# One mask product a head, float32r experts in the first feed-forward stage, and a rebuilt step order in the fourth attention

## The chip, the cores and the metric

The kernel runs on one core of one Trainium2 chip. The metric is the device time of one launch in microseconds (us). One core has five engines that work side by side and meet at semaphores: TensorE (PE in the rows), VectorE (DVE), ScalarE (ACT), GpSimd (POOL) and SyncE (SP, which issues DMAs).

## The reference, cut to what matters

Four transformer layers run one behind the other on x of shape (8, 256, 256): attention, normalisation, feed-forward, normalisation. The change touches three of the attentions and the first feed-forward stage.

```python
def _L0_ffn_ref(...):                       # 32 experts, 8 taken per token
    scores = jax.nn.sigmoid(logits)         # top 2 of 4 groups, then top 8 experts
    ...
    x_lat = x @ fc1_w.T
    h = relu2(jnp.einsum('tl,eil->eti', x_lat, w1))
    h = h * cw.T[:, :, None]
    y_lat = jnp.einsum('eti,eli->tl', h, w2)
    routed = y_lat @ fc2_w.T
    shared = relu2(x @ shared_up_w.T) @ shared_down_w.T
    return (shared + routed).reshape(orig_shape)

def _L1_attn_ref(...):                      # 16 heads of 128, causal
    scores = jnp.einsum('bhqd,bhkd->bhqk', q, k) * scale
    scores = jnp.where(mask[None, None], -jnp.inf, scores)
    attn = jax.nn.softmax(scores, axis=-1)
    ...

def _L3_attn_ref(...):                      # 16 heads, two score maps each, causal
    energy = jnp.einsum('bqhad,bkhad->bahqk', qd, kd)
    energy = jnp.where(causal, NEG, energy)
    scores = jax.nn.softmax(energy / np.sqrt(D), axis=-1)
    diff = scores[:, 0] - lam * scores[:, 1]
    diff = jnp.where(causal, NEG, diff)
    diff = jax.nn.softmax(diff, axis=-1)    # a second softmax
    att = jnp.einsum('bhqv,bvhd->bqhd', diff, v)
    att = att * jax.lax.rsqrt(jnp.mean(att * att, axis=-1, keepdims=True) + EPS) * rms_w
    return (att * (1.0 - LAM_INIT)).reshape(b, s, E) @ Wo
```

## The kernel before, in words

There are eight stages, named l0a, l0f, l1a, l1f, l2a, l2f, l3a and l3f (layer, then attention or feed-forward). x stays in SBUF as `x_sb`; between two stages a boundary normalises it and transposes it into `xT`. In each stage every engine has a program of its own, written by hand, and the order of the work is the order in which these programs are written, with semaphore waits between them.

**The masks.** A score tile of a head holds 128 query rows of the first half of the sequence against 128 keys, and 128 rows of the second half against 256 keys. The causal mask is added inside PSUM by a bf16 matrix product of the identity with a 128x128 mask tile: two products a head, of 128 columns each (L290 in l0a, L950 in l1a, L1836 in l3a). In l1a they stand between the score products (L948) of a group of two heads; there are 64 groups.

**l0f.** The 2048 tokens go in four chunks of 512, and each chunk runs over the 32 experts. For expert e, PE makes `hidden` = w1[e] times the latent tokens (L645, float32, which the trace records as two passes), and a product that spreads the expert's token weights over all partitions (L648, bf16). ScalarE takes relu (L687) and square (L689), VectorE multiplies by the weights (L757), and PE adds w2[e] times the result to the chunk's sum (`latent`, L652, float32), two experts behind. Before this loop stand the token routing (a long chain on VectorE) and the shared expert.

**l3a.** A batch of 256 tokens is handled in 8 steps, i=0 to i=7. A step makes one score map of 8 of the 32 (L1832), its maxima (VectorE L2090), its exponentials (ScalarE L1984, in two pairs of heads), and works on earlier maps: the ratio of the two softmaxes (L2097 to L2099), scaling, difference and mask (GpSimd L1947, L1950, L1937), the second maxima (L2106, L2108), the second exponentials (`second`, L2004), the transposes (`turn`, L1847) with their copies out of PSUM (L1995, L2116), the products with the values (L1857, L1860), the turning back (L1867) and the copy of the result (`take_output`, L2127). In between stand "pieces" for the next batch: projections (L1767, L1774, L1782) with their rotations on VectorE (L2055, L2058). Once a batch, the result of the batch before is squared (GpSimd L1954), normalised by three Newton steps on 128x32 tiles (L81 to L88) and a product (L2140), transposed (L1874), copied (L2010), projected (L1882), added to x (L108) and measured for the normalisation that follows (L115 to L121). Each engine's `sequence` function sets the order of a step; `live` says which parts exist while the pipeline fills and drains. `b` is the batch of the score maps, `piece_out` counts the pieces that VectorE has rotated, `on_raw` the results that it has taken.

## Time and profile before

| | |
|---|---|
| median of 3 runs | 3006.09 us (3003.32 to 3007.58) |
| the profiled execution | 2994.62 us, span 2992.8 us |
| PE busy | 2497.6 us (83%), mean granted clock 0.934 of full speed |
| VectorE busy | 1854.3 us (62%) |
| ScalarE busy | 1356.1 us (45%) |
| GpSimd busy | 461.8 us (15%) |
| l0f's expert loop | about 345 to 610 us of the span |
| l1a | about 660 to 1400 us |
| l3a | about 1957 to 2487 us |

Times in the rows are microseconds from the start of the span. The clock column of a stretch is TensorE's granted clock as a share of full speed. Busy shares are means over stages with different limits, so each stage has to be read by itself.

### The profile page before, as it was taken

The numbers are of one execution on the slowest core, as the hardware profiler recorded it, in microseconds if no ns is written. First come the engines' busy times: TensorE is split into PE (matmuls) and PEld (weight loads), VectorE is DVE, ScalarE is ACT, GpSimd is POOL, SyncE is SP. The second block draws the span as 40 slices with busy tenths as digits, with TensorE's granted clock in tenths as the row PEclk, the third lists the DMA queues.
The fourth block names the chain that finished last, engine by engine and source line by source line (L and its number), as shares of the span: only waits on it lengthen the run. The fifth ranks groups of instructions, "written<-read, shape, count | busy, mean of one in ns | idle before, by whom it ended". The sixth has DMA issues, their size and how long they took to land. (4 is left out here: it accounts for less than half of the span.)

```text
span 2992.8 us, 43034 instructions
## 1 busy us (share of the span) xinstructions
PE 2497.6 (83%) x14256; PEld 1870.0 (62%) x14256; DVE 1854.3 (62%) x4212; ACT 1356.1 (45%) x3688; POOL 461.8 (15%) x398
## 2 busy tenths in 40 slices
PE   7998999979999999995998786766666655999997
PEld 5665544457777777775676565654444434877876
DVE  3665333355675566756445757567777775777777
ACT  4664455554454444543222222267776762322332
POOL 2441000010000000000121000046565550000000
PEclk9998999989999999998999888889898866999999
DMA  4002000001110011102000000100000003000000
GB/s 154 7 11 85 1 0 0 0 4 32 32 32 17 14 32 32 32 21 105 1 0 0 0 0 0 35 17 4 7 4 4 4 1 138 1 0 0 0 0 28
DMA packets 28080, 63.74 MB, mean 21 GB/s; under 512 B 4208, under 2 KB 16496, under 8 KB 26480
## 3 DMA queue, kind: packets, MB, share of 16 engines
q1 hardware_dynamic: 28016, 62.93, 6.0%
q8 instruction: 35, 0.57, 0.1%
q14 instruction: 29, 0.24, 0.0%
HBM read 54.27 MB, written 2.10 MB: 19 GB/s over the span
## 5 line engine op out<-in xcount | busy, mean ns | idle before, releaser
L1984 ACT ACTIVATE l3a_pr<-psum,l3a_nm 128x128 f32<-128x128 f32 (+1 forms) x512 | 206.1, 420 | 90.5 <-DVE l3a_nm L2090 90.5
L757 DVE TENSOR_TENSOR l0f_hg<-l0f_sq,psum 128x512 f32<-128x512 f32 x128 | 87.7, 687 | 151.1 <-ACT l0f_sq L689 148.4
L108 DVE TENSOR_TENSOR x_sb<-psum,x_sb 128x512 f32 (+2 forms) x48 | 41.7, 868 | 219.7 <-PE psum L984 104.9
L2344 ACT ACTIVATE l3f_sg<-psum 128x512 f32<-128x512 f32 x96 | 57.3, 597 | 240.3 <-PE psum L2300 240.3
L1045 ACT ACTIVATE l1a_pr<-psum,l1a_nb,l1a_rq 128x128 f32<-128x128 f32 (+1 forms) x256 | 127.3, 510 | 85.2 <-DVE l1a_nb L1131 81.1
L2297 PE MATMUL psum<-l3f_x_hi,l3f_w_hi 128*128 x384 | 154.5, 402 | 8.6 <-DVE l3f_w_lo L2380 8.6
L2298 PE MATMUL psum<-xT,l3f_w_hi 128*128 x384 | 152.8, 398 | 0.0
L2299 PE MATMUL psum<-l3f_x_hi,l3f_w_lo 128*128 x384 | 152.1, 396 | 0.0
L2004 ACT ACTIVATE l3a_pr<-l3a_pr,l3a_nb,l3a_rec 128x128 f32<-128x128 f32 (+1 forms) x256 | 119.4, 542 | 68.5 <-DVE l3a_nb L2108 68.5
L1847 PE MATMUL psum<-cf_sb,l3a_pr 128*128 128x128 f32 x384 | 73.6, 312 | 82.3 <-ACT l3a_pr L2004 82.3
L2090 DVE TENSOR_REDUCE l3a_nm<-psum 128x2 f32<-128x256 f32 (+1 forms) x256 | 124.6, 548 | 24.5 <-PE psum L1836 21.8
L1305 POOL TENSOR_TENSOR l1f_acc<-l1f_t 128x512 f32<-128x512 f32 x4 | 6.3, 1573 | 855.7 <-DVE l1f_t L1368 855.7
L948 PE MATMUL psum<-l1a_kT,l1a_qT 128*128 128x128 f32 (+1 forms) x512 | 118.6, 355 | 21.0 <-ACT l1a_pr L1045 14.0
L2311 PE MATMUL psum<-l3f_w_hi,l3f_h_hi 128*128 128x256 f32 x384 | 126.5, 329 | 7.9 <-DVE l3f_h_lo L2398 7.9
L1947 POOL TENSOR_TENSOR l3a_pr<-l3a_pr,l3a_ratio 128x256 f32<-128x256 f32 (+1 forms) x128 | 103.2, 828 | 193.0 <-DVE l3a_ratio L2099 193.0
L1937 POOL TENSOR_TENSOR l3a_pr<-l3a_pr,w_l3a_mask 128x1024 f32<-128x1024 f32 x32 | 75.7, 2365 | 368.9 <-ACT l3a_pr L1984 368.9
L652 PE MATMUL psum<-l0f_hg,w_l0f_w 128*128 128x512 f32 x256 | 130.5, 593 | 0.8 <-DVE l0f_hg L757 0.8
L645 PE MATMUL psum<-l0f_xl,w_l0f_w 128*128 x256 | 130.6, 592 | 0.0
L687 ACT ACTIVATE l0f_relu<-psum 128x512 f32<-128x512 f32 x128 | 76.3, 596 | 108.7 <-PE psum L645 104.3
L374 POOL TENSOR_TENSOR l0a_pr<-l0a_pr,l0a_rec 128x256 f32<-128x256 f32 (+1 forms) x128 | 101.9, 828 | 144.2 <-DVE l0a_rec L464 144.2
L2391 DVE TENSOR_TENSOR l3f_gu<-l3f_sg,psum 128x512 f32<-128x512 f32 x96 | 66.0, 688 | 89.5 <-ACT l3f_sg L2344 89.5
L2328 ACT ACTIVATE l3f_w_hi<-w_l3f_all 128x768 fp32r<-128x768 f32 x97 | 82.2, 848 | 80.5 <-PE psum L2313 78.8
(445 smaller groups left out, 7198.9 us busy)
## 6 DMA issues: line engine op xcount, KB each, us to landing
l1a_kT<-l1a_o_dram SPq DMA_DIRECT2D x64, 256.0 KB, 2.7
w_l3f_all<-l3f_all_dram SPq DMA_DIRECT2D x1, 9216.0 KB, 25.7
w_l0f_w<-l0f_w_dram SPq DMA_DIRECT2D x2, 2048.0 KB, 10.1
w_l1f_all<-l1f_all_dram SPq DMA_DIRECT2D x1, 2560.0 KB, 9.5
cf_sb<-xT SPq DMA_DIRECT2D x9, 256.0 KB, 2.5
x_sb<-x_dram SPq DMA_DIRECT2D x1, 2048.0 KB, 8.6
l0a_xc<-xT SPq DMA_DIRECT2D x8, 256.0 KB, 2.5
w_l1a_q<-l1a_q_dram SPq DMA_DIRECT2D x1, 2048.0 KB, 8.1
```

The costliest lines, as they stand in the source:

```text
L645: mm(HB[e % 3], w["w1"][:, e, :], xl[:, chunk], start=True, stop=True).then_inc(h_ps, 1)
L652: mm(YL, w["w2"][:, e, :], hg[:, e % 2, :], start=(e == 0), stop=(e == E - 1)).then_inc(used, 1)
L948: mm(S[n % 2][:, i, t * P:t * P + (t + 1) * P], qT[:, h, t * P:(t + 1) * P], kT[:, h, 0:(t + 1) * P], start=True, stop=False)
L1045: last = nc.scalar.activation(pr[:, n % 2, i, s], S[n % 2][:, i, s], ACT.Exp, bias=nb[:, n % 2, t, i:i + 1], scale=rq[:, t, 2 * n + i:2 * ...
L1947: last = nc.gpsimd.tensor_tensor(pr[:, r, 1, heads, k], pr[:, r, 1, heads, k], bc(ratio[:, r, heads, t], 2, (t + 1) * P), ALU.mult)
L1984: last = nc.scalar.activation(pr[:, r, a, g, k], S[:, g, k], ACT.Exp, bias=nm[:, i % 2, g, t:t + 1], accum_out=sums[:, r, a, g, t:t + 1])
L2004: last = nc.scalar.activation(pr[:, r, 1, g, k], pr[:, r, 0, g, k], ACT.Exp, bias=nb2[:, r, g, t:t + 1], scale=rec[:, r, 0, g, t:t + 1])
L2090: last = nc.vector.tensor_reduce(nm[:, i % 2, 2 * pair:2 * pair + 2, t], S[:, 2 * pair:2 * pair + 2, t * P:t * P + (t + 1) * P], AX.X, ALU ...
L2297: mm(bk[e % 2], hi, x_hi[:, k, chunk], start=(k == 0), stop=False)
L2298: mm(bk[e % 2], hi, x_lo[:, k, chunk], start=False, stop=False)
L2299: mm(bk[e % 2], lo, x_hi[:, k, chunk], start=False, stop=(k == KD - 1))
L2311: mm(Y[:, t, :], h_hi[:, e % 2, tokens], hi, start=False, stop=False)
```

## The change

Six things are done together.

1. Each head's two mask products become one of 256 columns: its output is a view of the bank, `diagonals(bank)`, that holds both diagonal blocks. In l1a the four score products of a group now come first and its two mask products last.
2. In l0f, w1 and w2, the latent tokens and the gated hidden values are split into a float32r part (`_hi`) and its remainder (`_lo`), and each float32 product becomes three float32r products: hi·hi, hi·lo and lo·hi. w's hi parts are made by ScalarE between the steps of the shared expert (8 pieces of 128x1024), the lo parts by GpSimd (8 pieces), xl_hi by ScalarE, xl_lo by VectorE (4 products ahead of the top-k chain). In the loop relu, square and the multiplication work in place in four buffers `act_h`; h_hi of even experts is copied by ScalarE, that of odd ones by VectorE; h_lo is a VectorE subtraction. `latent` runs three experts behind instead of two.
3. To make room, l1a's v weights (2 MB) are loaded in the boundary ahead of l1a instead of one boundary earlier, third in the queue behind q and k.
4. In l3a VectorE makes the second maxima right behind the maxima. The sums of the norm stand at i=5, the Newton steps and the product in i=6 ahead of its copy out of PSUM, and their `rs` lies in PSUM, so that each Newton operation reads at most one operand from SBUF. Squares move from i=3 to i=2.
5. In l3a the output projection of a batch, its addition to x and its measure move from i=7 of the next batch to i=0 and i=1 of the batch after that. ScalarE's copy `output` comes behind both pairs of exponentials instead of between them.
6. In l3a the pieces move: queries 3 from i=0 to i=3, values from i=4 to i=5, queries 2 from i=6 to i=7; the piece stands ahead of both transposes instead of between them, and at i=4 the turning back stands between the two transposes, with its result taken at the end of the same step.

```diff
-                        for t in range(TT):
-                            last = mm(S[:, g, 2 * t * P:(2 * t + 1) * P], c["idb"], c["maskb"], start=False, stop=(t == TT - 1))
+                        last = mm(diagonals(S[:, g, :]), c["idb"], bc(c["maskb"], 1, TT), start=False, stop=True)
...
                     def hidden(e):
                         if e >= 3:
-                            pe.wait_ge(sq_ready, b * E + e - 2)
-                        mm(HB[e % 3], w["w1"][:, e, :], xl[:, chunk], start=True, stop=True).then_inc(h_ps, 1)
+                            pe.wait_ge(relu_ready, b * E + e - 2)
+                        mm(HB[e % 3], w_hi["w1"][:, e, :], xl_hi[:, chunk], start=True, stop=False)
+                        mm(HB[e % 3], w_hi["w1"][:, e, :], xl_lo[:, chunk], start=False, stop=False)
+                        mm(HB[e % 3], w_lo["w1"][:, e, :], xl_hi[:, chunk], start=False, stop=True).then_inc(h_ps, 1)
...
+                        nc.scalar.activation(act_h[:, e % 4, :], act_h[:, e % 4, :], ACT.Square).then_inc(sq_ready, 1)
+                        if e % 2 == 1:
+                            act.wait_ge(hg_ready, b * E + e)
+                            if e >= 4:
+                                act.wait_ge(used, b * E + e - 3)
+                            nc.scalar.activation(h_hi[:, (e - 1) % 3, :], act_h[:, (e - 1) % 4, :], ACT.Copy).then_inc(hhi_even, 1)
...
+                        nc.vector.tensor_tensor(act_h[:, e % 4, :], act_h[:, e % 4, :], GB[e % 2], ALU.mult).then_inc(hg_ready, 1)
+                        if e >= 1:
+                            low(e - 1)
+                        if e % 2 == 1:
+                            dve.wait_ge(hg_ready, b * E + e + 1)
+                            if e >= 3:
+                                dve.wait_ge(used, b * E + e - 2)
+                            nc.vector.tensor_copy(h_hi[:, e % 3, :], act_h[:, e % 4, :]).then_inc(hhi_odd, 1)
...
-        rs = sb("rs", [P, TT * H])
+        rs = PT[1][:, 3 * P:3 * P + TT * H]
...
                 def sequence(b, opening=False, second_pass=False, closing=False, more=True):   # VectorE
+                    behind = not (opening or second_pass)
                     for i in range(NU):
                         if not closing:
                             maxima(b, i)
                             if i == 7 and more:
-                                add_keys(b * NQ + 8)
+                                add_keys(b * NQ + 7)
+                        if live(i, 3, opening, closing):
+                            second_maxima(b, i)
                         if i % 2 == 0 and live(i, 1, opening, closing):
                             ratios(b, i)
                         if i % 2 == 0 and live(i, 6, opening, closing):
                             values_out(b, i)
-                        if i % 2 == 1 and live(i, 7, opening, closing):
+                        if i == 0 and behind:
+                            output(b - 2)
+                        if i in (1, 3, 7) and live(i, 7, opening, closing):
                             if i == 7 and not opening:
                                 dve.wait_ge(on_ready, b)
                             take_output(b, i)
-                        if not closing and i < 7:
+                        if not closing:
                             piece_in(b, i, more)
+                        if i == 5 and not opening:
+                            norm_1(b - 1)
                         if live(i, 4, opening, closing):
                             out_of_psum(b, i, opening)
-                        if live(i, 3, opening, closing):
-                            second_maxima(b, i)
-                        if not opening:
-                            if i == 6:
-                                norm_1(b - 1)
-                                norm_2(b - 1)
-                            if i == 7:
-                                output(b - 1)
-                                dve.wait_ge(z_ready, b + 1)
-                                measure(nc, st, x_sb, mv, b * TT - TT, TT, lw)
+                        elif i == 6 and closing:
+                            norm_2(b - 1)
+                        if i == 4 and not opening:
+                            take_output(b, i)
+                        if i == 1 and behind:
+                            dve.wait_ge(z_ready, b - 1)
+                            measure(nc, st, x_sb, mv, b * TT - 2 * TT, TT, lw)
```

How the change moves instructions is shown at three places. First PE in l0f's expert loop, from one expert's weight product to the next; `w_l0f_w` and `l0f_w_hi`, `l0f_w_lo` are the weights, `l0f_c3T` the token weights. Before:

```order
L648 MATMUL psum<-l0f_c3T,w_l0f_sel 128x512
L652 MATMUL psum<-l0f_hg,w_l0f_w 128x512
L645 MATMUL psum<-l0f_xl,w_l0f_w 128x512
L647 REGISTER_ALU
L648 MATMUL psum<-l0f_c3T,w_l0f_sel 128x512
```

Now:

```order
L666 MATMUL psum<-l0f_c3T,w_l0f_sel 128x512
L670 MATMUL psum<-l0f_h_hi,l0f_w_hi 128x512
L671 MATMUL psum<-l0f_h_hi,l0f_w_lo 128x512
L672 MATMUL psum<-l0f_h_lo,l0f_w_hi 128x512
L661 MATMUL psum<-l0f_xl_hi,l0f_w_hi 128x512
L662 MATMUL psum<-l0f_xl_lo,l0f_w_hi 128x512
L663 MATMUL psum<-l0f_xl_hi,l0f_w_lo 128x512
...
L666 MATMUL psum<-l0f_c3T,w_l0f_sel 128x512
```

One float32 product of 512 columns has become three float32r products, twice for each expert.

Second, VectorE in l3a's looped pass, at the end of step i=6 and in i=7. Before:

```order
L2106 TENSOR_REDUCE l3a_nm<-l3a_pr 128x2 x2
...
L2108 TENSOR_TENSOR l3a_nb<-l3a_nm,l3a_rec 128x4
L2134 TENSOR_REDUCE l3a_vv<-l3a_osq 128x32
...
L81 TENSOR_SCALAR l3a_rs<-l3a_vv 128x32
...
L84 TENSOR_TENSOR l3a_tmp<-l3a_rs 128x32
...
L2140 TENSOR_TENSOR l3a_on<-l3a_raw,l3a_rs 128x512
...
L2090 TENSOR_REDUCE l3a_nm<-psum 128x2 x2
...
L2065 TENSOR_TENSOR l3a_kr<-l3a_k 128x512
L2127 COPY l3a_raw<-psum 128x8x17
L2116 COPY l3a_pt<-psum 128x384
L2106 TENSOR_REDUCE l3a_nm<-l3a_pr 128x2 x2
...
L108 TENSOR_TENSOR x_sb<-psum,x_sb 128x512
```

Now (L2167 are the maxima, L2183 and L2185 the second ones, L2217 to L2222 the norm):

```order
L2167 TENSOR_REDUCE l3a_nm<-psum 128x2 x2
...
L2183 TENSOR_REDUCE l3a_nm<-l3a_pr 128x2 x2
...
L2185 TENSOR_TENSOR l3a_nb<-l3a_nm,l3a_rec 128x4
...
L2200 COPY l3a_ots<-psum 128x256
L2217 TENSOR_SCALAR psum<-l3a_vv 128x32
...
L2219 SCALAR_TENSOR_TENSOR l3a_tmp<-psum,l3a_vv 128x32
...
L2222 TENSOR_TENSOR l3a_on<-l3a_raw,psum 128x512
L2195 COPY l3a_pt<-psum 128x384
...
L2167 TENSOR_REDUCE l3a_nm<-psum 128x2 x2
...
L2183 TENSOR_REDUCE l3a_nm<-l3a_pr 128x2 x2
...
L2185 TENSOR_TENSOR l3a_nb<-l3a_nm,l3a_rec 128x4
L2206 COPY l3a_raw<-psum 128x8x17
```

The norm's operations have moved ahead of the copy L2195, the second maxima stand right behind the maxima, and the addition to x (L108) is gone from i=7.

Third, PE in the same pass, in i=7 and at the start of the next batch. Before:

```order
L1832 MATMUL psum<-l3a_kr,l3a_qr 128x128 x4
L1832 MATMUL psum<-l3a_kr,l3a_qr 128x256 x4
L1836 MATMUL psum<-cb_sb 128x128 x8
L1847 MATMUL psum<-cf_sb,l3a_pr 128x128 x3
L1874 MATMUL psum<-cf_sb,l3a_on 128x128 x4
L1847 MATMUL psum<-cf_sb,l3a_pr 128x128 x3
L1882 MATMUL psum<-l3a_wo,l3a_oT 128x256 x4
```

Now:

```order
L1888 MATMUL psum<-l3a_kr,l3a_qr 128x128 x4
L1888 MATMUL psum<-l3a_kr,l3a_qr 128x256 x4
L1891 MATMUL psum<-cb_sb 128x2x128 x4
L1902 MATMUL psum<-cf_sb,l3a_pr 128x128 x6
L1929 MATMUL psum<-cf_sb,l3a_on 128x128 x4
L1834 MATMUL psum<-xT,w_l3a_q 128x256 x4
...
L1888 MATMUL psum<-l3a_kr,l3a_qr 128x128 x4
```

The output projection (L1882) has left i=7, and a projection of queries (L1834) has come there, behind the transposes and ahead of the next batch's scores.

## Rows read from the trace of the kernel before

**Rows 1.** Busy time by stretch: span, PE, weight loads, VectorE, ScalarE, GpSimd, clock, DMA.

```profile
345.00:610.00 265.00, 255.60 (x666) 113.03 (x665) 101.03 (x169) 156.47 (x256) 0.00 (x0) 1.00 0.00 0
```

**Rows 2.** The same view for one batch of l3a and its closing pass.

```profile
2065.90:2129.00 63.10, 40.28 (x384) 29.14 (x383) 48.73 (x115) 44.85 (x172) 37.56 (x29) 0.91 0.01 4
...
2445.30:2487.00 41.70, 21.10 (x102) 13.49 (x101) 17.62 (x58) 14.07 (x39) 7.91 (x7) 0.57 0.00 0
```

**Rows 3.** Waits in l3a, 2012.9 to 2445.3: total us, times, longest.

```profile
ACT l3a_pr L1984 <- DVE l3a_nm L2090: 65.5, 15, 6.8
ACT l3a_pr L2004 <- DVE l3a_nb L2108: 57.2, 49, 2.2
```

**Rows 4.** Timeline of one plain step of l3a: start, us, [idle before <-releaser].

```profile
2159.40 0.35 ACT L1984 ACTIVATE l3a_pr<-psum,l3a_nm 128x128 f32<-128x128 f32 x1
...
2161.86 0.69 DVE L2058 TENSOR_TENSOR l3a_qr<-psum,w_l3a_rope_q 128x512 f32<-128x512 f32 x1 [1.99 <-PE psum L1774]
...
2162.74 0.94 PE L1832 MATMUL psum<-l3a_kr,l3a_qr 32*128 32x128 f32 x16 [0.60 <-ACT l3a_pr L1984]
...
2163.97 0.16 DVE L2108 TENSOR_TENSOR l3a_nb<-l3a_nm,l3a_rec 128x4 f32<-128x4 f32 x1
2164.08 1.95 DVE L2090 TENSOR_REDUCE l3a_nm<-psum 128x2 f32<-128x256 f32 x4
...
2164.16 1.86 ACT L2004 ACTIVATE l3a_pr<-l3a_pr,l3a_nb,l3a_rec 128x128 f32<-128x128 f32 x4 [1.09 <-DVE l3a_nb L2108]
...
2165.93 0.35 ACT L1984 ACTIVATE l3a_pr<-psum,l3a_nm 128x128 f32<-128x128 f32 x1
```

**Rows 5.** Timeline around the norm of one batch, VectorE, GpSimd and PE apart.

```profile
2184.89 1.68 DVE L84 TENSOR_TENSOR l3a_tmp<-l3a_rs 128x32 f32<-128x32 f32 x1
2186.61 2.26 DVE L86 SCALAR_TENSOR_TENSOR l3a_tmp<-l3a_vv,l3a_tmp 128x32 f32<-128x32 f32 x1
...
2189.13 0.19 DVE L84 TENSOR_TENSOR l3a_tmp<-l3a_rs 128x32 f32<-128x32 f32 x1
...
2198.11 0.69 DVE L108 TENSOR_TENSOR x_sb<-psum,x_sb 128x512 f32 x1 [2.68 <-PE psum L1882]
...
2186.49 2.33 POOL L1937 TENSOR_TENSOR l3a_pr<-l3a_pr,w_l3a_mask 128x1024 f32<-128x1024 f32 x1
...
2191.23 1.12 PE L1874 MATMUL psum<-cf_sb,l3a_on 128*128 128x128 f32 x4 [5.12 <-DVE l3a_on L2140]
...
2194.49 3.46 PE L1882 MATMUL psum<-l3a_wo,l3a_oT 128*128 128x256 f32 x8 [1.50 <-ACT l3a_oT L2010]
```

**Rows 6.** Timeline of l0f's expert loop.

```profile
599.78 0.60 ACT L687 ACTIVATE l0f_relu<-psum 128x512 f32<-128x512 f32 x1 [0.68 <-PE psum L645]
...
600.66 1.02 PE L645 MATMUL psum<-l0f_xl,w_l0f_w 128*128 x2
...
601.13 0.69 DVE L757 TENSOR_TENSOR l0f_hg<-l0f_sq,psum 128x512 f32<-128x512 f32 x1 [1.25 <-ACT l0f_sq L689]
...
602.60 1.02 PE L645 MATMUL psum<-l0f_xl,w_l0f_w 128*128 x2
```

**Rows 7.** Timeline of l3f, which already has float32r products and roundings.

```profile
2704.69 0.40 PE L2297 MATMUL psum<-l3f_x_hi,l3f_w_hi 128*128 x1
...
2704.92 0.43 DVE L2396 CAST l3f_h_hi<-l3f_hw 128x512 fp32r<-128x512 f32 x1
...
2705.38 0.69 DVE L2398 TENSOR_TENSOR l3f_h_lo<-l3f_hw,l3f_h_hi 128x512 fp32r<-128x512 f32 x1
2705.39 0.40 PE L2297 MATMUL psum<-l3f_x_hi,l3f_w_hi 128*128 x1
...
2705.99 0.95 DVE L2380 TENSOR_TENSOR l3f_w_lo<-w_l3f_all,l3f_w_hi 128x768 fp32r<-128x768 f32 x1
```

**Rows 8.** Timeline of PE in one group of l1a: its first score product, and what follows.

```profile
705.17 0.39 PE L948 MATMUL psum<-l1a_kT,l1a_qT 128*128 128x128 f32 x2
...
706.87 0.82 PE L959 MATMUL psum<-cf_sb,l1a_pr 128*128 128x128 f32 x6
```

More of the change, by code:

```diff
@@ L1822, in scores @@
+                def scores(b, i, opening, more):
                     r, a = i // A, i % A
@@ new lines, in sequence @@
+                            if i in (2, 4) and more and not closing:
+                                pe.wait_ge(piece_out, b * NQ + (6 if i == 2 else 8))
+                            if i == 6:
+                                pe.wait_ge(piece_out, b * NQ + (11 if more else 7))
+                            values(b, i)
+                        if i == 0 and behind:
+                            if closing:
+                                pe.wait_ge(on_raw, b * R - 3)
+                            else:
+                                pe.wait_ge(piece_out, b * NQ + 5)
+                            project_output(b - 2)
@@ L1896, in sequence @@
+                        if not closing and i < 7:
+                            piece(b, i, opening, more)
                         if turning:
                             turn(b, i, 0)
[L1898 to L1911 removed]
@@ L2145, in output, with sequence @@
                     add_output(nc, x_sb, b * TT, TT, OB.rearrange("p (t n) -> p t n", t=TT), z_ready)
-                def sequence(b, opening=False, closing=False, more=True):
+                def sequence(b, opening=False, second_pass=False, closing=False, more=True):
+                    behind = not (opening or second_pass)
                     for i in range(NU):
```

299 lines of the change are left out of this document (183 added, 116 removed).

## Prediction

> **What bounds the kernel now.** I read the busy times by stretch first, since the three parts of the change lie in stages with different limits. In l0f's expert loop [rows 1] PE is busy for 255.6 of 265 us at the full clock while ScalarE has 156.5 and VectorE 101.0: PE is the bound. The timeline says how: one expert's first product starts at 600.66 and the next one's at 602.60, so an expert takes 1.94 us [rows 6], and both other engines wait in it for PE or for each other.
>
> In l3a nobody is full. One batch takes 63.1 us, with VectorE busy for 48.7, ScalarE 44.9, PE 40.3 and GpSimd 37.6 [rows 2]. So I looked at the waits: from 2012.9 to 2445.3, ScalarE waits 65.5 us for the first maxima in 15 waits of up to 6.8, and 57.2 us for the second maxima (L2108) in 49 short ones [rows 3]. These are two different faults.
>
> The short one stands in a plain step, which lasts 6.53 (from 2159.40 to 2165.93) [rows 4]. VectorE has the next score maxima only after second maxima that stand behind a rotation, which waited 1.99 for PE's projection; ScalarE then idles 1.09 before its second exponentials, which end just when the next step begins.
>
> The long ones come once a batch, at the norm [rows 5]. The Newton steps stand ahead of the maxima of i=7. Two 128x32 operations take 1.68 and 2.26 beside GpSimd work (L1937 runs from 2186.49 for 2.33), and the same operation takes 0.19 at 2189.13, once GpSimd is done. PE has by then stood still for 5.12. After that the output projection takes 3.46 for 8 products, VectorE waits 2.68 for it in L108, and the score products of the next batch stand behind it. This is the second of the waits of several us.
>
> **l0f, part by part.** An expert had two float32 products and a bf16 one, and gets six float32r products and the bf16 one. In l3f three float32r products of 512 columns take 0.70 (from 2704.69 to 2705.39), 0.233 each [rows 7]. Seven make 1.63 against 1.94: 0.31 less, times 128 experts 39.7.
>
> Do the others keep up? VectorE gets, for two experts, two multiplications, two subtractions and a cast. A subtraction lasts 0.69 in its record, but the next instruction starts 0.61 behind it (2705.38 to 2705.99), and the cast lasts 0.43 [rows 7]. By starts it is 4 x 0.61 + 0.46 = 2.90, by whole records 4 x 0.69 + 0.43 = 3.19, that is 1.45 or 1.60 an expert. ScalarE's 256 instructions were busy for 156.5 [rows 1], 0.61 each; five for two experts are 1.53 an expert. Both are under 1.63, so PE stays the bound, but barely: all three are within 12%. I take 1.63, with 1.70 as the worse end (a wait of 0.14 in each pair), which costs 9 us.
>
> At a chunk's end the last expert's chain is laid bare. It gains a cast (0.46), its own subtraction (0.61) and the subtraction of the expert before it that stands ahead (0.61), and gets back 0.3 on shorter products: about +1.3, four times, 5.2. Ahead of the loop ScalarE rounds the weights in 8 pieces of 1024 columns between the steps of the shared expert. At 0.61 for 512 columns they are 9 us of work; PE has three banks ahead of ScalarE there, so I take +1 of it as shown, between 0 and 9. And VectorE's four subtractions go ahead of a routing chain. GpSimd's 8 pieces of the weights run beside that chain; it is the one place where the change puts GpSimd work beside VectorE work that had none. If that chain grew by up to 5 us, it would still end ahead of the shared expert, which PE finishes; if that cover were gone, 5 us would show. Sum for l0f: -39.7 + 5.2 + 1 = -33.5, between -17 (the worse end of each) and -40.
>
> **l3a, the plain steps.** With second maxima right behind the maxima, ScalarE's work for its second exponentials is ready while it makes the first ones. What is left of a step is a loop over ScalarE, PE and VectorE: exponentials and the way to PE 3.34 (2159.40 to 2162.74), score products 0.87, half the mask products 0.16, half of the maxima 0.93 to 1.0 and the way to ScalarE, together 2.3 [rows 4]. That is 5.65 for a step, 45.2 for a batch: the floor. ScalarE itself needs 44.9/8 = 5.6, VectorE 48.7/8 = 6.1 less the stalls in its own records (3.6 a batch), so 5.65 too [rows 2, 5]. Three engines are then at one level, and any wait in order shows.
>
> I went through the new order step by step and put each step at the floor or at what comes late. At i=0 the turning back waits for the addition to x, which waits for the projection (+0.6). At i=1 VectorE also measures (+0.4). At i=2 the turning back waits for a rotation of keys (+0.6). At i=3 PE has two projections, and the second waits for a result taken in the same step by VectorE: the next scores come late (+1.5). i=4 is +0.3, i=5 with the norm's sums and two pieces +1.1. At i=6 VectorE has Newton's ten operations (about 2.2 at the 0.19 of [rows 5] with the gaps between them) and the product: +1.9. At i=7 the projection of queries 2 waits for a result that VectorE takes behind the sum of the keys, and stands ahead of the next batch's scores: +2.4. The sum is 45.2 + 8.8 = 54.0, against 63.1: -9.1, for seven batches -64. Where the additions are all half as large, a batch is 49.6; where the waits at i=3, i=7 and i=0 are twice as large, 58.5. The first batch has no norm and gains only from the plain order, about -3. In the closing pass, 41.7 us at a mean clock of 0.57 [rows 2], the last ratio no longer stands behind the addition to x and its 2.68 of waiting [rows 5]; but the moved projections must still be made. I take -7, between 0 and -10. Sum for l3a: -74, between -40 and -105.
>
> **The norm and GpSimd, weighed.** The rows show a factor of 9 to 12 between the same operation beside GpSimd work and without it [rows 5]. They do not show whether operands in PSUM help. With `rs` in PSUM I cost the Newton steps at the free price; if they don't help, they cost 3.6 more in each of seven batches, +25. The Trainium skill, "SBUF — State Buffer", section "Who interferes with whom", says that a VectorE instruction with two SBUF inputs contends with a GpSimd instruction that reads SBUF, and that with at most one it does not; the trace agrees for the two inputs (1.68 and 2.26 against 0.19), and for the single input no row here shows it. The same rule speaks against the change where two SBUF inputs stay: the sum of the keys, the second operation of the norm's sums, L2185, and the routing of l0f beside the new GpSimd work. By it the Newton steps are free and these may each cost up to one GpSimd instruction.
>
> **The masks and the rest.** A group's four score and four mask products take 1.70 (705.17 to 706.87) [rows 8]. Their columns alone need 1.28 (768 float32 columns, at 0.85 for 512: half of the 1.94 that is left without the bf16 product) and 0.23 for 512 bf16 ones, so 0.19 is lost between eight products. The edit saves at most that in a group, at least nothing; I take 0.09 for 64 groups: -5.5, between 0 and -12. In l0a the same edit stands off the limiting chain: -0.3. The later load of v is third in its queue, and ScalarE and PE are still on q and k when it lands; I take 0, and 8 us if it isn't hidden.
>
> **Sum.** -33.5 - 74 - 5.5 - 0.3 = -113. From the profiled execution's 2994.6 that gives 2881. The median of the runs shown is 11.5 higher; scaled to it, 2893.
>
> **The rivals.**
> - The new waits of PE in l3a (i=3, i=7, i=0) are as large as the old ones, and a batch takes 58 to 61. For it: PE waits for VectorE in the same step three times, where it waited once. Against it: the 5.12 and 3.46 are gone from the path. At 59.5 l3a gives -36, all -75: about 2931, or 2917 at 57.5. Chance 0.25.
> - The steps reach nearly the floor, 49 to 50.5: l3a -105, all -144: 2862. Chance 0.15.
> - The stall stays although `rs` lies in PSUM: +25, 2918. Chance 0.04.
> - l0f becomes bound by VectorE and ScalarE at 1.70 or more: 2902 to 2906. It is within my own range. Chance 0.08.
> - Slower or no change: TensorE gets its lower level, half the clock, in l0f's loop. A product then costs 0.47, an expert 3.3. At that price the gain of 113 is gone once about 0.53 of the 128 experts run so (113/(128 x 1.66)). In its favour, the float32r products last barely longer than the others need; against it, PE had 1.00 there and stays busy [rows 1]. Chance 0.03.
> - My forecast, a batch of 52 to 57 and an expert at 1.61 to 1.66: 2872 to 2912. Chance 0.45.
>
> **The numbers.** 2893 is the likeliest. The two ends come from the first two rivals: 2855 and 2935 leave out about 0.15. A median can be told from no change at about 0.2%, 6 us here. Faster 0.97, within it 0.01, slower 0.02.
>
> **What would show it.** In the profile after: an expert's first products 1.63 apart with PE over 95% busy, or 1.70 with gaps; l3a's batches from i=7 to i=7 at 54 with ScalarE's waits for first maxima spread over i=3, i=6 and i=7, none above 3; its waits for L2185 near zero; Newton operations at 0.2 beside running GpSimd work; an output projection at i=0 that no engine waits for by more than 1. The prediction is wrong if batches stay above 58, if the second maxima now wait for GpSimd's difference, or if l0f's experts are over 1.75.

## The result: 0.978 of the time before, half to six tenths of the gain that was forecast

The changed kernel takes 2937.5 us in the median of 4 runs (2936.46 to 2944.65), and the kernel before 3004.7 in the median of the runs beside it: a ratio of 0.9777 with a 95% interval of 0.9759 to 0.9794. It is faster, by 67 us. The forecast was 2893, in a range of 2855 to 2935, so the measured time lies just outside. By the medians that is six tenths of the 113 that were forecast. The profiled executions are 2994.62 and 2937.16 us, 57.5 apart, which is half of it; the one of before is 11.5 under its median.

Where the 57.5 came from can be read from the first and last starts of the same products in both traces. l1a's first score product starts at 654.9 instead of 681.7: l0f gave 26.8 (forecast 33.5). From l1a's first to its last score product it is 666.1 instead of 671.8: 5.7 (forecast 5.5). From l3a's first score product to l3f's first expert product it is 547.8 instead of 570.1: 22.3, where 74 were forecast. The stages between and behind have the rest, under 3. The miss is in l3a. Inside these 22.3, by the starts of the first exponentials, the first batch gave 0.9, the six batches behind it 8.4 together, the last one, up to its i=7, 6.6, and what follows up to l3f 6.3. So seven batches gave 15 us where 64 were forecast.

The stretches of the profile after, one chunk of l0f's loop, the start of the next, and one batch of l3a; the columns are those of [rows 1]:

```profile
345.40:403.20 57.80, 55.43 (x233) 38.07 (x232) 48.51 (x82) 45.80 (x80) 0.00 (x0) 1.00 0.00 1
403.20:408.30 5.10, 2.98 (x13) 1.75 (x11) 3.88 (x14) 2.35 (x4) 0.00 (x0) 1.00 0.00 0
408.30:414.00 5.70, 5.66 (x18) 3.79 (x18) 4.44 (x8) 4.61 (x8) 0.00 (x0) 0.70 0.00 0
...
2162.20:2223.60 61.40, 43.90 (x349) 31.14 (x349) 48.84 (x114) 44.20 (x169) 37.93 (x29) 0.83 0.01 4
```

A batch of l3a takes 61.4 us instead of 63.1 [rows 2], with the same work on VectorE and ScalarE and TensorE's mean granted clock at 0.83 instead of 0.91. The waits from 1978 to 2400, nearly seven batches, in the columns of [rows 3]:

```profile
ACT l3a_pr L2059 <- DVE l3a_nm L2167: 86.0, 55, 4.7
PE psum L1834 <- DVE l3a_raw L2206: 45.6, 13, 5.2
...
PE psum L1922 <- DVE l3a_ots L2200: 30.9, 16, 2.7
...
ACT l3a_pr L2079 <- DVE l3a_nb L2185: 5.8, 6, 1.0
```

The waits for the second maxima are gone (5.8 instead of 57.2), as the change meant them to be. But ScalarE waits for its first maxima by 86.0 instead of 65.5, now in 55 waits instead of 15. And there is a new row: PE waits 45.6 for the copy L2206 ahead of the projection of queries L1834, once at i=7 and once at i=3 of nearly every batch. The worst place is i=7, in time order:

```profile
2211.00 1.94 DVE L2167 TENSOR_REDUCE l3a_nm<-psum 128x2 f32<-128x256 f32 x4
2211.67 0.60 PE L1929 MATMUL psum<-cf_sb,l3a_on 128*128 128x128 f32 x4
...
2212.86 2.12 DVE L2138 TENSOR_TENSOR l3a_kr<-l3a_k 128x512 f32<-128x512 f32 x1
2214.38 2.79 POOL L2012 TENSOR_TENSOR l3a_pr<-l3a_pr,w_l3a_mask 128x1024 f32<-128x1024 f32 x1
2214.90 1.00 DVE L2183 TENSOR_REDUCE l3a_nm<-l3a_pr 128x2 f32<-128x256 f32 x2
...
2215.93 1.27 DVE L2185 TENSOR_TENSOR l3a_nb<-l3a_nm,l3a_rec 128x4 f32<-128x4 f32 x1
2217.12 0.29 DVE L2206 COPY l3a_raw<-psum 128x136 f32<-128x136 f32 x1
...
2217.46 3.78 PE L1834 MATMUL psum<-xT,w_l3a_q 128*128 x8 [5.20 <-DVE l3a_raw L2206]
2221.18 1.03 PE L1888 MATMUL psum<-l3a_kr,l3a_qr 32*128 32x128 f32 x16
```

VectorE has the maxima at 2212.9, then makes the sum of the keys in 2.12 us, the second maxima, L2185 in 1.27, and only then the copy of 0.29 for which PE waits. PE stands still for 5.20, and its projection then takes 3.78 for 8 products. The scores of the next batch come behind it, at 2221.18. From the first exponentials of i=7 to those of i=0 it is 11.57 us (2212.05 to 2223.62).

### The profile page after: what moved, and what is told of

Read it like the earlier page. It is cut to its first block and busy times, and to the rows that moved or that the text cites. A ratio compares the mean times of both kernels' runs of the same rounds, so it can differ in the third digit from the quotient of the medians.

```text
span 2935.4 us, 42983 instructions
## 1 busy us (share of the span) xinstructions
PE 2473.6 (84%) x14000; PEld 1912.8 (65%) x14000; DVE 1958.4 (67%) x4408; ACT 1389.4 (47%) x3760; POOL 483.6 (16%) x406
## 5 line engine op out<-in xcount | busy, mean ns | idle before, releaser
L2167 DVE TENSOR_REDUCE l3a_nm<-psum 128x2 f32<-128x256 f32 (+1 forms) x256 | 124.7, 550 | 50.5 <-PE psum L1891 50.1
L1834 PE MATMUL psum<-xT,w_l3a_q 128*128 (+1 forms) x256 | 84.2, 488 | 48.8 <-DVE l3a_raw L2206 47.9
L1007 PE MATMUL psum<-l1a_kT,l1a_qT 128*128 128x128 f32 (+1 forms) x512 | 100.6, 342 | 22.7 <-ACT l1a_pr L1105 15.7
L1044 PE MATMUL psum<-l1a_kT,l1a_ko 128*128 128x256 f32 x512 | 112.6, 381 | 6.1 <-ACT l1a_ko L1094 6.1
L2025 POOL TENSOR_TENSOR l3a_pr<-l3a_pr 128x768 f32<-128x768 f32 x64 | 115.7, 1808 | 5.0
L1635 PE MATMUL psum<-w_l2f_down,l2f_hh 128*128 128x256 f32 x256 | 73.5, 457 | 47.9 <-DVE l2f_hh L1703 47.9
L2059 ACT ACTIVATION_READ_ACCUMULATOR l3a_pr<-psum,l3a_nm 128x1 f32 x512 | 110.6, 216 | 0.0
```

The lines of the kernel that those rows point to most:

```text
L1044: last = mm(PT[0][:, t * D:(t + 1) * D], oT[:, h, t * P:(t + 1) * P], wo[:, h, :], start=(h == 0), stop=(h == H - 1))
L2025: nc.gpsimd.tensor_tensor(pr[:, r, 0, heads, :], pr[:, r, 0, heads, :], pr[:, r, 1, heads, :], ALU.add).then_inc(dif_ready, 1)
L2059: last = nc.scalar.activation(pr[:, r, a, g, k], S[:, g, k], ACT.Exp, bias=nm[:, i % 2, g, t:t + 1], accum_out=sums[:, r, a, g, t:t + 1])
L2167: last = nc.vector.tensor_reduce(nm[:, i % 2, 2 * pair:2 * pair + 2, t], S[:, 2 * pair:2 * pair + 2, t * P:t * P + (t + 1) * P], AX.X, ALU ...
```

## The experiments

The times of before beside the experiments were 3003.6 to 3006.0 in the median. Ratios are those to before of the same chip. Twelve kernels ran.

**1. The parts apart.** The changed kernel with the fourth attention's old order, so with l0f and the masks alone. The edit exchanges the whole function `l3_attention` for that of the kernel before, with one mask product a head.

> The changed kernel with the fourth attention's old order (its mask products stay merged). It leaves the gains of l0f and of the masks. The trace of the changed kernel has l1a's first score product 26.8 us earlier and l1a itself 5.7 us shorter. If the parts are additive: 3004.7 - 26.8 - 5.7 - 2 = about 2970, and the step order of l3a is worth about 32 us less than nothing else: 2937 - 2970 = -33. If l3a's rebuilt order is worth only what lies between its first score product and l3f (22 us), this kernel takes 2960.

Measured: 2972.4 us (2965.4 to 2974.2), ratio 0.9894 (0.9877 to 0.9910). The forecast of 2970 holds. l0f and the masks are worth 32 us, and the rebuilt order of l3a the other 35. The 22 us that the two profiled executions gave for l3a are no contradiction: from l3a's first score product to l3f's first expert product the old order takes 570.1 in the trace of before and 576.9 in the trace of this kernel, so single executions of the same order differ by 7 us.

**2. The masks alone,** on the kernel before; the cut shows l0a and l3a, and in l1a the two mask products of a group also move behind its four score products:

```diff
-                        for t in range(TT):
-                            last = mm(S[:, g, 2 * t * P:(2 * t + 1) * P], c["idb"], c["maskb"], start=False, stop=(t == TT - 1))
+                        last = mm(diagonals(S[:, g, :]), c["idb"], bc(c["maskb"], 1, TT), start=False, stop=True)
```

> The kernel before with only the merged mask products in l0a, l1a and l3a. Theory: 5.7 us in l1a, nothing in l0a, and in l3a little, since ScalarE and VectorE set its step: 2998, a gain of 5 to 9. Rival: in l3a the scores reach VectorE 0.2 us earlier in each of 64 steps, another 13: 2986.

Measured: 2994.5 us (2984.0 to 3002.6), ratio 0.9965 (0.9945 to 0.9985): 4 to 17 us. The forecast 2998 lies in it, the rival's 2986 just outside. It is faster. In its trace l1a, from its first to its last score product, is 6.6 us shorter than before, while l3a is 10.7 longer up to l3f's first expert product, so nothing here shows that l3a gained.

**3. The copy first.** The changed kernel, with VectorE's copy right behind the maxima at i=3 and i=7, nothing else moved (the second hunk takes it out of its old place):

```diff
                         if not closing:
                             maxima(b, i)
-                            if i == 7 and more:
-                                add_keys(b * NQ + 7)
+                        if i in (3, 7) and live(i, 7, opening, closing):
+                            if i == 7 and not opening:
+                                dve.wait_ge(on_ready, b)
+                            take_output(b, i)
+                        if i == 7 and more and not closing:
+                            add_keys(b * NQ + 7)
                         if live(i, 3, opening, closing):
                             second_maxima(b, i)
...
-                        if i in (1, 3, 7) and live(i, 7, opening, closing):
-                            if i == 7 and not opening:
-                                dve.wait_ge(on_ready, b)
+                        if i == 1 and live(i, 7, opening, closing):
                             take_output(b, i)
```

> The changed kernel, but at i=3 and i=7 of l3a VectorE takes the turned-back result right behind the maxima, ahead of the sum of the keys and the second maxima. Theory 'order': the batch of 61.45 us is long because PE's projection at i=7 waits 5.2 us (and at i=3 1.1 us) for that copy, then runs at the lower clock (3.78 instead of 1.99) ahead of the next scores. The copy comes about 4.3 and 2.3 us earlier, so a batch loses 5 to 6.5: 2892 to 2902. Theory 'ports': the sum of the keys (2.12 us) and L2185 (1.27) stay as long beside GpSimd work and hold the next maxima instead: at most 1.5 a batch, 2927 or more.

Measured: 2888.6 us (2885.0 to 2892.5), ratio 0.9611 (0.9593 to 0.9630). That is 49 us less than the changed kernel, from the place of one instruction of 0.29 us in two of eight steps. A batch is down from 61.4 to 54.75: i=7 is 4.4 shorter, i=3 2.3, and the other steps are as they were within 0.2. The place at i=7 now reads:

```profile
2131.14 1.94 DVE L2167 TENSOR_REDUCE l3a_nm<-psum 128x2 f32<-128x256 f32 x4
2132.18 0.37 ACT L2059 ACTIVATE l3a_pr<-psum,l3a_nm 128x128 f32<-128x128 f32 x1 [1.78 <-DVE l3a_nm L2167]
2132.99 0.29 DVE L2206 COPY l3a_raw<-psum 128x136 f32<-128x136 f32 x1
2133.20 1.92 DVE L2138 TENSOR_TENSOR l3a_kr<-l3a_k 128x512 f32<-128x512 f32 x1
...
2133.34 1.99 PE L1834 MATMUL psum<-xT,w_l3a_q 128*128 x8 [1.08 <-DVE l3a_raw L2206]
...
2135.56 0.94 PE L1888 MATMUL psum<-l3a_kr,l3a_qr 32*128 32x128 f32 x16 [0.23 <-ACT l3a_pr L2059]
```

The sum of the keys is nearly as slow as it was (1.92 instead of 2.12), yet PE no longer waits for it. PE waits 1.08 instead of 5.20, its projection takes 1.99 instead of 3.78, and the scores wait for ScalarE's exponentials by 0.23, as they should. The mean clock of a batch is 0.94. Theory "order" holds, and theory "ports" falls: with the stalls still there the batch lost 6.7, not 1.5. That the stalls cost nothing at all doesn't follow: i=7 still takes 7.2, and the maxima of the next step start at 2138.34, behind these operations, while PE's mask products ended at 2137.04.

**4. Two of the three stalls beside GpSimd taken away instead,** on the changed kernel. L2185 becomes four operations with one SBUF input and a scalar each, and the norm's second operation reads one input from PSUM. For this the norm's sums also move behind the wait for the transpose. The third stall, that of the sum of the keys, stays:

```diff
-                    nc.vector.tensor_tensor(nb2[:, r, heads, :], nm2[:, r, heads, :], rec[:, r, 0, heads, :], ALU.mult).then_inc(nb_ready, 1)
+                    for g in range(heads.start, heads.stop):
+                        for t in range(TT):
+                            last = nc.vector.tensor_scalar(nb2[:, r, g, t:t + 1], nm2[:, r, g, t:t + 1], rec[:, r, 0, g, t:t + 1], None, ALU.mult)
+                    last.then_inc(nb_ready, 1)
...
-                    st.do(nc.vector.tensor_reduce(by_head(vv[:, :]), osq[:, :, :, 0:HD], AX.X, ALU.add))
+                    st.do(nc.vector.tensor_reduce(by_head(tv), osq[:, :, :, 0:HD], AX.X, ALU.add))    # tv in PSUM, vv in SBUF
```

> The changed kernel, but L2185 (two SBUF inputs, 1.27 to 1.35 us beside GpSimd work, 0.16 alone) is made of four operations with one SBUF input and a scalar each, and the norm's second operation (2.24 us at i=5, 0.21 alone) reads one input from PSUM. Theory 'ports': the waits of 1.1 at i=7, 1.2 at i=3 and 2.0 at i=5 go, 4 us a batch, 2908 to 2915. Theory 'order': only what brings the copies at i=3 and i=7 forward counts, 2.3 less 0.3 for three more operations, 2921 to 2926. Should the operations with one input be stalled too, no change.

Measured: 2939.7 us (2938.3 to 2940.4), ratio 0.9782 (0.9765 to 0.9798): no gain. The two stalls themselves did go. The four operations and the norm's second one over the whole run:

```profile
L2188 DVE TENSOR_SCALAR l3a_nb<-l3a_nm,l3a_rec x256: 202/204/216, 1947.3 to 2413.6; 128x1 f32<-128x1 f32 x128
...
L2220 DVE SCALAR_TENSOR_TENSOR l3a_vv<-l3a_osq,psum x8: 204/208/210, 2018.7 to 2422.5; 128x32 f32<-128x32 f32 x8
```

The longest of 256 is 216 ns, and the norm's operation has 208 ns in the median, where the changed kernel has 2233. But four operations last 0.58 together where the one lasted 0.16 unless it was stalled, in every one of 64 steps, and PE still waits 4.46 for the copy at i=7, behind the sum of the keys at 2.12. So the equal time is a sum of gains and prices, and not a proof that the stalls were free. In most batches of the trace i=3 takes 7.7 instead of 8.5 and i=1 is 0.3 shorter, while i=0, i=2 and i=6, where L2185 had taken its 0.16, are 0.4 longer each; the mean batch is 61.5 in both kernels. What the stall of the sum of the keys costs in this order was not measured by itself.

**5. Both edits together:**

> Both edits of the two runs before: copies first at i=3 and i=7, and L2185 and the norm's second operation with one SBUF input. With the long wait gone, the batch is 54.75 us and VectorE stands on more of its steps, so a stall of VectorE should now show. Theory 'ports show once the order is mended': the 2.24 at i=5 becomes 0.2 and L2185's stalls go: 2 to 3 us a batch, 2868 to 2875. Rival: as in the changed kernel, where the same edit gave nothing, the time is in PE's waits: 2885 to 2892.

Measured: 2895.7 us (2895.4 to 2896.1), ratio 0.9642 (0.9612 to 0.9672). By the medians that is 7 us more than experiment 3, against my expectation, but the two ran on different chips and the intervals of their ratios overlap, so a loss isn't shown. In the trace the steady batches are in fact shorter: the third to the seventh take 54.0, 55.2, 53.6, 52.6 and 53.9 us, where experiment 3 has 54.7 each time. i=0, i=2 and i=6 are 0.4 longer, which is the price of the four operations, but i=7 is 0.7 shorter and i=5 takes 5.7 in four of the five, where experiment 3 has 7.1 to 7.6. So by the trace the stalls do cost something once the order is mended: 0.9 a batch beyond the price of the four operations.

What is longer is the second batch (55.5 instead of 53.2) and the last (50.4 instead of 45.4). At i=3 of the last one PE waits for its copy about as long in both kernels, but the projection behind the wait takes 3.78 here:

```profile
2324.86 3.78 PE L1835 MATMUL psum<-xT,w_l3a_q 128*128 128x256 f32 x8 [1.82 <-DVE l3a_raw L2212]
```

and 1.99 in experiment 3:

```profile
2323.56 1.99 PE L1834 MATMUL psum<-xT,w_l3a_q 128*128 128x256 f32 x8 [2.03 <-DVE l3a_raw L2206]
```

The granted clock behind the wait is 0.50 here and 1.00 there. Why it differs isn't shown.

**6. Keep PE busy through the wait.** The changed kernel with unread products ahead of the wait at i=7:

```diff
                     if i == 7 and more:
+                        for _ in range(40):
+                            mm(PT[1][:, 4 * P - 64:4 * P], c["idb"], c["maskb"][:, 0:64], start=True, stop=True)
                         pe.wait_ge(on_raw, b * R + 1)
```

> The changed kernel with 40 small bf16 products that nobody reads, put by PE at i=7 of l3a ahead of its wait for the copy, into columns of a bank that nothing else uses. The wait stays, only PE isn't still in it. Theory 'the lower clock is a third of the loss': the projection behind the wait takes 2.0 instead of 3.78, and the scores 0.94 instead of 1.03: 1.8 us for seven batches, 2923 to 2927. Rival: the clock falls anyway, or what is won is waited away at VectorE: 2935 to 2940.

Measured: 2938.6 us (2936.8 to 2939.8), ratio 0.9785 (0.9754 to 0.9815). This one told nothing of the clock: the 40 products took 1.33 us, a wait of 4.18 was left, and the projection still took 3.68. So it was run again with 140.

> The changed kernel with 140 of the unread bf16 products at i=7. With 40 they took 1.3 us, left a wait of 4.2, and the projection behind it still took 3.7: the test didn't keep PE busy. 140 take about 4.7 of the 5.5 us. Theory 'the lower clock is part of the loss': the projection takes 2.0, -1.7 us in seven batches: 2924 to 2929. Rival: 2936 to 2940, if what it wins is waited for elsewhere; longer if the products outlast the wait.

Measured: 2931.9 us (2927.1 to 2932.5), ratio 0.9761 (0.9729 to 0.9794). The stretches of the products and of the projection there, and under them the wait and the projection of the changed kernel:

```profile
2211.80:2217.20 5.40, 4.25 (x142) 4.12 (x139) 5.37 (x7) 4.37 (x19) 5.09 (x3) 1.00 0.00 0
2217.20:2219.30 2.10, 2.04 (x12) 1.56 (x14) 0.01 (x2) 1.69 (x4) 0.00 (x0) 1.00 0.00 0
```

```profile
2212.30:2217.40 5.10, 0.00 (x0) 0.00 (x0) 5.07 (x7) 4.11 (x19) 4.80 (x3) 0.72 0.00 0
2217.40:2221.20 3.80, 3.74 (x12) 2.55 (x12) 0.01 (x1) 1.70 (x4) 0.00 (x0) 0.50 0.00 0
```

With PE idle for 5.2 us the granted clock is 0.50 in the projection, which is 1.2 GHz; kept busy but for the last 1.21 us it is 1.00, and the same 8 products take 1.99 us. The step i=7 is 1.8 to 2.0 shorter in six of the seven batches that have these products, 11.3 together, but the medians differ by 5.6 only. Part of the rest stands at i=3, which is 1.6 longer in four of these batches: in the long run's trace the second projection there waits 2.74 for its copy and takes 2.69, where the changed kernel has 1.06 and 1.99. The intervals of the two ratios overlap, so the clock's effect on the projection is shown, and its worth in the whole only about.

**7. rs in SBUF again,** on the changed kernel:

```diff
-        rs = PT[1][:, 3 * P:3 * P + TT * H]
+        rs = sb("rs", [P, TT * H])[:, :]
```

> The changed kernel with the norm's rs in SBUF again, so that the Newton operations have two SBUF inputs. Theory: they stand beside GpSimd's L2022 and L2025 at i=6, so they wait for these, about 3.3 us in each of seven batches ahead of the maxima of i=7: 2955 to 2962. Rival: the wait is swallowed by PE's later wait for the copy: 2937 to 2945.

Measured: 2980.1 us (2975.7 to 2989.3), ratio 0.9921 (0.9897 to 0.9944): 43 us slower than the changed kernel, twice what I expected. The Newton steps of i=6:

```profile
2164.21 0.97 DVE L2219 SCALAR_TENSOR_TENSOR l3a_tmp<-l3a_rs,l3a_vv 128x32 f32<-128x32 f32 x1
2165.22 1.87 POOL L2025 TENSOR_TENSOR l3a_pr<-l3a_pr 128x768 f32<-128x768 f32 x1
2165.22 0.19 DVE L2220 TENSOR_TENSOR l3a_tmp<-l3a_rs,l3a_tmp 128x32 f32<-128x32 f32 x1
2165.45 1.69 DVE L2221 SCALAR_TENSOR_TENSOR l3a_rs<-l3a_tmp,l3a_rs 128x32 f32<-128x32 f32 x1
...
2168.73 1.85 POOL L2025 TENSOR_TENSOR l3a_pr<-l3a_pr 128x768 f32<-128x768 f32 x1
2168.73 0.19 DVE L2221 SCALAR_TENSOR_TENSOR l3a_rs<-l3a_tmp,l3a_rs 128x32 f32<-128x32 f32 x1
2168.96 1.68 DVE L2219 SCALAR_TENSOR_TENSOR l3a_tmp<-l3a_rs,l3a_vv 128x32 f32<-128x32 f32 x1
2170.55 2.33 POOL L2012 TENSOR_TENSOR l3a_pr<-l3a_pr,w_l3a_mask 128x1024 f32<-128x1024 f32 x1
2170.67 2.26 DVE L2220 TENSOR_TENSOR l3a_tmp<-l3a_rs,l3a_tmp 128x32 f32<-128x32 f32 x1
```

An operation that starts where a GpSimd instruction ends takes 0.19, and the next one in these rows lasts about as long as the GpSimd instruction beside it. The ten operations last from 2163.72 to 2173.15, 9.4 us, where the changed kernel has 2.2. In the new order they stand in the middle of GpSimd's work, so without the PSUM placement the step i=6 takes 14.4 us instead of 7.2. The batch is 68.3 instead of 61.5, since i=3 is 1.4 longer too and i=7 1.8 shorter.

**8. All rounding of h in l0f on VectorE,** on the changed kernel (the counts that the subtraction waits for follow, not shown):

```diff
-                        if e % 2 == 1:
-                            act.wait_ge(hg_ready, b * E + e)
...
-                            nc.scalar.activation(h_hi[:, (e - 1) % 3, :], act_h[:, (e - 1) % 4, :], ACT.Copy).then_inc(hhi_even, 1)
...
-                        if e % 2 == 1:
+                        if True:
                             dve.wait_ge(hg_ready, b * E + e + 1)
```

> The changed kernel with all h_hi casts of l0f's loop on VectorE. Starts of VectorE's instructions are 0.61 + 0.61 + 0.46 = 1.68 us an expert against PE's 1.63. Theory: VectorE becomes the bound by 0.05 for 128 experts, about 6 us, and each chunk's end changes little: 2942 to 2947. Rival: VectorE's cast waits for its own product, 0.1 to 0.2 each: 1.85 an expert, 2960 to 2966.

Measured: 2942.4 us (2941.4 to 2943.6), ratio 0.9796 (0.9766 to 0.9826): 5 us more than the changed kernel by the medians, with intervals that overlap. VectorE's rows there stand back to back, where in the changed kernel every second product waits 0.29 for ScalarE:

```profile
541.45 0.68 DVE L793 TENSOR_TENSOR l0f_h_lo<-l0f_act_h,l0f_h_hi 128x512 fp32r<-128x512 f32 x1
542.05 0.42 DVE L806 CAST l0f_h_hi<-l0f_act_h 128x512 fp32r<-128x512 f32 x1
542.47 0.69 DVE L799 TENSOR_TENSOR l0f_act_h<-l0f_act_h,psum 128x512 f32<-128x512 f32 x1
543.07 0.68 DVE L793 TENSOR_TENSOR l0f_h_lo<-l0f_act_h,l0f_h_hi 128x512 fp32r<-128x512 f32 x1
```

An expert takes 1.62 us (541.45 to 543.07), which is PE's own 1.63, with VectorE full. The size came out as expected, but not its reason: the loop isn't slower in this stretch. In the two traces the whole loop, by the starts of its first products (L661), is 1.6 longer here; where the rest of the 5 us is, if it is real, stays open.

**9 to 11. Can the mended order be improved?** Three kernels on top of experiment 3: the norm's one-input edit alone, the copy of the values (L2200) ahead of the second maxima at even steps, and both. The second edit, without the lines that it takes out of the old place:

```diff
+                        if i % 2 == 0 and live(i, 6, opening, closing):
+                            values_out(b, i)
                         if live(i, 3, opening, closing):
                             second_maxima(b, i)
```

> The kernel with copies first (2888.6 us), and of the one-input edits only that of the norm, which costs no instruction more. Before it, the run with both edits was 7 us slower than copies first, and its L2185 took 0.58 for four operations instead of 0.16 in every step. Theory 'four operations cost more than the stalls': this kernel loses nothing and gains what L2214's stall was (0.92 at i=5 less 0.21), up to 0.7 a batch: 2884 to 2889. Rival, that the place of the norm's sums behind the wait for the transpose costs: 2893 or more.

> Copies first, and at even steps also the copy of the values (L2200) ahead of the second maxima. In the trace of copies first, PE waits 2.67 us for it at i=4, and the score products behind it take 1.67 instead of 0.94. The copy comes 1.7 us earlier. Theory 'what PE waits for must be first on VectorE': i=4 to i=5 falls from 7.07 to about 6.1 and i=6 by 0.5: 1.5 us a batch, 2876 to 2881. Rival: scores are held by the exponentials (p_exp) there, only the clock gains 0.7: 2883 to 2886.

> Copies first at i=3 and i=7, the copy of the values first at even steps, and the norm's second operation with one SBUF input: the sum of the two runs beside it. If their gains add, 2873 to 2880. If both shorten the same wait at i=6, it is as fast as the better of the two.

Measured: the norm alone 2891.2 us (2888.8 to 2897.9), ratio 0.9635 (0.9610 to 0.9660); the values first 2888.2 (2884.8 to 2892.4), 0.9620 (0.9595 to 0.9645); both 2883.8 (2881.4 to 2886.4), 0.9605 (0.9581 to 0.9630). Against experiment 3's 2888.6 none of them can be told from no change by the intervals. In the trace of the values first, PE's wait at i=4 is down from 2.67 to 0.98, and the scores behind it wait 1.28 for the exponentials, as the rival had it. The step i=4 is shorter all the same, 5.7 instead of about 7.1 in four of the five steady batches, so the wait did hold it; i=1 and i=7 give back 0.2 and 0.35, and i=3 0.9 or 1.0 in three of the five. The whole shows no gain. The last kernel has the lowest median of all and is clearly faster than both kernels of this case, but not clearly than experiment 3.

## Why the prediction was wrong, step by step

**The step that failed: i=7 of l3a.** The prediction had "at i=7 the projection of queries 2 waits for a result that VectorE takes behind the sum of the keys, and stands ahead of the next batch's scores: +2.4". It named the right place and the right queue, and mis-sized it: the term measured 5.9 (11.57 less the floor of 5.65). The prediction doesn't say what the 2.4 is made of, and ahead of the copy it names only the sum of the keys. Against free prices three things are larger or new: the second maxima, which the change had put ahead of the copy, 2.2 with L2185 at 1.27 instead of 0.16; the sum of the keys at 2.12 instead of 0.68, as long as the operations in [rows 5] that stood beside GpSimd work; and the projection at half the clock, 3.78 instead of 1.99. Experiment 3 shows that the place in VectorE's queue is the cause: with the copies first i=7 is 4.4 shorter and i=3 2.3, and the long wait is gone. The clock was for the most part a consequence: holding it up at i=7 alone gave about a tenth of what the order gave (experiment 6's second kernel, 5.6 against 49). The stalls are only in part priced: two of the three away gave nothing before the order was mended (experiment 4), the third was never taken away.

**The other steps of l3a.** Time from the first exponentials of a step to those of the next, in one steady batch of each trace, with the forecast for the changed kernel (before has batches of 62.7 and of 63.5):

| step | before | forecast | changed | experiment 3 |
|---|---|---|---|---|
| i=0 | 6.86 | 6.25 | 6.39 | 6.39 |
| i=1 | 6.54 | 6.05 | 6.80 | 6.81 |
| i=2 | 6.64 | 6.25 | 6.42 | 6.37 |
| i=3 | 6.53 | 7.15 | 8.48 | 6.18 |
| i=4 | 6.06 | 5.95 | 6.94 | 7.07 |
| i=5 | 6.82 | 6.75 | 7.64 | 7.50 |
| i=6 | 13.33 | 7.55 | 7.23 | 7.22 |
| i=7 | 9.93 | 8.05 | 11.57 | 7.21 |
| batch | 62.7 | 54.0 | 61.5 | 54.75 |

So the norm's move won 6.1 at i=6, as forecast, and i=3, i=4, i=5 and i=7 gave back 5.3 of it. Of the 7.5 by which the batch misses the forecast, i=7 has 3.5, i=3 1.3, i=4 1.0, i=5 0.9 and i=1 0.75. i=3 has the same fault as i=7 on a smaller scale: its copy stands behind L2185 at 1.35, and the first of its two projections takes 3.37 at a clock of 0.55. At i=5 the norm's second operation took 2.24. That experiment 3 comes out near the 54.0 of the forecast is luck in part: its i=3 and i=7 are 1.0 and 0.8 under their forecast, and i=1, i=4 and i=5 0.75 to 1.1 over theirs. The first rival (58 to 61, "the new waits of PE in l3a (i=3, i=7, i=0) are as large as the old ones") was what happened, a little beyond its end, and it had a chance of 0.25: the new wait at i=7 is 5.20, the old one was 5.12. The prediction's own signs said so too: batches above 58, and a wait for the first maxima of 4.7 where none was to be above 3.

**The norm.** Right: with rs in PSUM the Newton operations take 0.19 to 0.20 beside running GpSimd work, and PE's wait for the norm (5.12 in [rows 5]) no longer stands among its waits. The price of the rival, "3.6 more in each of seven batches", was half of what the operations cost in the new order (7.2 at i=6; experiment 7). It was taken from the old place of these operations, where GpSimd ran beside two of them only.

**The rule of two SBUF inputs** (the Trainium skill, "SBUF — State Buffer", section "Who interferes with whom"). For single inputs from SBUF no row that the prediction shows bears on it; experiments 4 and 7 do: 0.21 instead of 2.23 with one input, and up to 2.26 instead of 0.19 with two. The prediction gives the rule without the exception that the same section makes, for operations in a two-port mode. The trace of before has a row that the short form doesn't cover; that it is a case of the exception isn't shown. L81 reads one input from SBUF and writes to SBUF, and in the second batch it lasts as long as the GpSimd instruction that starts with it:

```profile
2058.26 1.81 POOL L1950 TENSOR_TENSOR l3a_pr<-l3a_pr 128x768 f32<-128x768 f32 x1
2058.26 1.84 DVE L81 TENSOR_SCALAR l3a_rs<-l3a_vv 128x32 int32<-128x32 int32 x1
```

Elsewhere it takes 0.18, in experiment 7 it has 0.46 in the median, and with its result in PSUM it never takes more than 0.20. What the rule says against the change was there too, in L2138, L2185 and L2214.

**l0f.** The steady expert is right: 1.63 us, from the first product of one (545.13) to that of the next (546.77) and of the one after (548.38). The chunk is 57.8 instead of 65.4, 7.6 less where 8.6 were forecast. The loop as a whole, up to the last chunk's projection behind it (L682, L662 before), is 28.0 shorter, where 128 experts at 0.31 would give 39.7, so 11.7 are lost where the forecast had 5.2. By the starts of the weight products (L666, L648 before) they go to three places. The chunk ends cost 1.7 to 1.85 each, not 1.3, about 6.9 together. The first five experts of a chunk gain 0.6 to 0.65 less than five times 0.31, which the forecast put at nothing, about 2.4. And in two of the four chunks the clock falls at the start: in the second chunk PE waits 2.16 for VectorE's first product, the granted clock then is 0.70 between 408.3 and 414.0, and the same float32r products start 0.43 apart instead of 0.23. That costs 1.1 there and 1.4 in the third chunk, by comparison with the fourth, where PE waits 2.13 and the clock stays at 1.00. Before, PE was idle for 1.7 at the same places and the clock stayed at 1.00. So the rival "TensorE gets its lower level" happened at two chunks' starts alone. Of the 6.5 beyond the forecast's 5.2 the ends have 1.7, the starts 2.4 and the clock 2.5. No run changes any of them by itself.

**The rest.** l1a gave 5.7 against 5.5, the closing pass of l3a about 6 against 7, the first batch 0.9 against 3. The v weights and the routing hid as forecast: l0f's loop starts at 345.4 instead of 344.4 and l1a's gain is whole.

## What to carry to other kernels

When work is moved so that one engine gets ahead, read for every instruction that another engine waits for what now stands in front of it on its own engine, and put the short copy that releases a long chain first: here a copy of 0.29 us, placed first in two of eight steps, was worth 49 us. Mend the longest wait first and price the stalls again afterwards: taking two of them away left the batch at 61.5 in the old order and took 0.9 off it in the mended one. And a fix for a stall has a price of its own: four free operations in place of one that stalled now and then cost 0.4 in each of three steps where it hadn't stalled, so compare step by step, not only the stalled place.

## What the runs showed of the hardware

- A VectorE operation of 128x32 that reads two SBUF inputs takes 0.19 us alone and up to 2.26 beside a GpSimd instruction; the same with one input from PSUM stayed at 0.19 to 0.21 in every occurrence. One with a single SBUF input and its result in SBUF (L81) took 1.84 once in the trace of before and 0.18 elsewhere there, while 256 operations of 128x1 with a scalar from SBUF stayed at 0.22 or less (experiment 4). Ten dependent operations took 9.4 us instead of 2.2, seven of them longer than 0.4 (experiment 7).
- After 5.2 us without a product TensorE's granted clock was 0.50 in the next 3.8 us, and 8 projections took 3.78 us; with unread small products through the wait it was 1.00, and they took 1.99. The length of the idle stretch alone doesn't tell what follows. In l0f the clock was 0.70 behind 2.16 at one chunk's start and 1.00 behind 2.13 at another's; at i=3 of l3a's last batch it was 0.50 behind 1.82 (experiment 5) and 1.00 behind 2.03 (experiment 3).
- 40 products of 64 bf16 columns take 1.33 us and 140 take 4.25, 0.03 each: much less than I had taken for them, and the reason why the first try told nothing.
